# Attention stage of a graph network kernel: order of the first loads on SP, and the engine that clears the accumulator

## The chip, the cores and the metric

One core of a Trainium2 chip runs the whole program in one launch. The metric is the device time of that launch in microseconds: the median of three runs is 8271.29 us (8269.59 to 8273.54).

## The reference, cut to what matters

The program computes a layer stack on 6250 nodes of 256 features and 200,000 edges: a heterogeneous graph attention, a mixing branch, a routed feed-forward part, then a graph convolution, a linear attention and a mixture of experts. The change lies in the edge part of the first of these:

```python
q_att = jnp.einsum('nhd,rhde->rnhe', q, relation_att)
v_msg = jnp.einsum('nhd,rhde->rnhe', v, relation_msg)
aw_q_edge = q_att[etype, col_idx]
msg_edge = v_msg[etype, row_idx]
attn_score = jnp.sum(aw_q_edge * k[row_idx], axis=-1)
score = attn_score * (relation_pri[etype] / SQRT_DK)
m = jax.ops.segment_max(score, col_idx, num_segments=n)
ex = jnp.exp(score - m[col_idx])
denom = jax.ops.segment_sum(ex, col_idx, num_segments=n)
alpha = ex / denom[col_idx]
agg = jax.ops.segment_sum(alpha[..., None] * msg_edge, col_idx, num_segments=n)
```

The kernel folds the relation matrices into a table with one row for each relation and source node (keys and values, 2 KB a row), so each edge gathers one row of that table and is multiplied with the query of its target node. Edges are sorted by target.

## The kernel before, in words

The program is a row of stages (function `stage`), each followed by a barrier of all engines (line 3014 in the profile) and the clearing of its semaphores. The stage before the changed one, `node_tables`, writes the table and the queries to HBM. The changed stage is `attention_edges`; after it come `merge_carried` and `after_attention`.

`attention_edges` works on 208 groups (GROUPS) of 8 tiles (G) of 128 edges. Four slots (SLOTS) hold groups in flight: group k uses slot k mod 4. Targets are held in 50 blocks (NB) of 126 nodes, and all 50 blocks of queries (`qb`, 128 x 256 f32 each, 128 KB) and of accumulators (`acc`, 128 x 13300 f32 in all) stay in SBUF.

- **SP** loads. Lines 1026 and 1027: the block numbers of all steps (`blocks`, every second of 1664 integers, 832 pieces of 4 bytes, written over the start of `step_sums`). Line 1029: the fifty blocks of queries. Line 1031 (`chunk_load`): the edge columns of 16 groups at a time (192 KB), double-buffered. Lines 1039 and 1043 (`rows`): for each group the places of its edges, broadcast to 128 partitions (`oht`, 512 KB), and a mask (32 rows of 129 f32). A row load waits for the expansion of the group that last used its slot, a mask load for its weighting.
- **POOL** clears `acc` (line 1069) and then issues the gathers (line 1065), eight a group, 128 rows of 2 KB each. Each group's gathers wait for its index copy on ACT; from the fifth group on, every second gather also waits for one of the four summed pairs of the group four before it (`sum_made`), because they share a slot.
- **ACT** goes through a fixed order (`in_turns`): for a position k it does the copies and the store of group k-1's sums, the exponents and the one-hot places of group k, then `columns` and `mark` of group k+1, `indices` of group k+4 and `nodes` of group k+3. So before the loop the order is indices 0; indices 1, nodes 0; indices 2, nodes 1; columns 0, mark 0, indices 3, nodes 2. `mark` (lines 1192 and 1193) waits for the scores of its group. `indices` is line 1216, the sum copies are line 1173.
- **PE** waits for all queries (`q_in`, 50 loads) and for the packed block numbers (`packed_ready`), then goes through look-ups, expansions (line 1252: one-hot times query block, 16 matmuls a group), transposes of scores (1261) and of maxima (1269, 1270), and sums (line 1283, 16 matmuls in four pairs). An expansion waits for the node places of its group and for DVE's multiply of the group before.
- **DVE** first negates a column (1148), waits for `cleared` and for `blocks_in`, packs the block numbers (lines 974 to 977) and signals PE (1152). Then for each group: multiply gathered keys by expanded queries (line 1108, waits for all eight gathers and the expansion), reduce to scores (1130), two scans for the running maximum (1117, 1121), weights (1135), weighted values (1144), and the four additions into `acc` (line 1102) of the group before.

Of the kernel before, what the change touches and what calls it, by code (L numbers as in the profile page):

```python
# [20 lines left out]
P = 128  # L21
# [5 lines left out]
NB = 50  # L27
BW = 126
# [951 lines left out]
def attention_edges(nc, sem, psum, bank, c, dram):  # L980
# [3 lines left out]
    with ExitStack() as ctx:  # L984
# [6 lines left out]
        qb = sbt("q", [P, NB, D])  # L991
# [31 lines left out]

        @block.sync
        def _(sp):
            sp.dma_start(blocks, dram["blocks"].rearrange("(m x) -> m x", x=2)[:, 0:1].rearrange("m x -> x m"),
                         allow_slow_non_contiguous=True).then_inc(blocks_in, 16)
            for b in range(NB):
                sp.dma_start(qb[:, b, :], dram["q"][b * BW:b * BW + P, :]).then_inc(q_in, 16)
            def chunk_load(n):  # L1030
                sp.dma_start(chunk[:, (n % 2) * CHUNK:(n % 2 + 1) * CHUNK].rearrange("p k c g -> p (k c g)"),
                             dram["cols"][:, n * CHUNK:(n + 1) * CHUNK].rearrange("p k c g -> p (k c g)")
                             ).then_inc(chunk_in, 16)

            def rows(i):
                for s in range(SLOTS):
                    k = i * SLOTS + s
                    wait_count(sp, expanded[s], i)
                    sp.dma_start(oht[:, s, :], dram["rel_rows"][bass.ds(k * G, G)].rearrange("g n -> (g n)")
                                 .unsqueeze(0).broadcast_to([P, G * P])).then_inc(rows_in[s], 16)  # L1040

                    wait_count(sp, weighted[s], i * 2)
                    sp.dma_start(mk[:, s, :], dram["mask"][bass.ds(k * G, G)].rearrange("g h n -> (g h) n")
                                 ).then_inc(loaded[s], 16)
            chunk_load(0)
            for n in range(GROUPS // CHUNK):
                first = n * CHUNK // SLOTS
                rows(first)
                if n + 1 < GROUPS // CHUNK:
                    sp.wait_ge(chunk_in, 16 * n + 16)  # L1050

                    wait_count(sp, col_ready, CHUNK * n)
                    wait_count(sp, index_ready, CHUNK * n)
                    chunk_load(n + 1)
                with sp.Fori(first + 1, first + CHUNK // SLOTS) as i:
                    rows(i)
            sp.wait_ge(sum_added, GROUPS * PACK)
            for a, b in ((0, 112), (112, BW)):
                sp.dma_start(dram["sums"][0:NB * BW].rearrange("(b p) n -> p b n", p=BW)[a:b], acc[a:b]).then_inc(acc_stored, 16)
            sp.wait_ge(acc_stored, 32)  # L1060

        @block.gpsimd
        def _(g):
            def gather(i, s, n):
                g.indirect_dma_start(out=kv[:, s, n, :], out_offset=None, in_=dram["table"],  # L1065
                                     in_offset=bass.IndirectOffsetOnAxis(ap=index[:, s, n:n + 1].bitcast(U32), axis=0)
                                     ).then_inc(gathered[s], 16)

            g.memset(acc[:], 0.0).then_inc(cleared, 1)
            for s in range(SLOTS):  # L1070
                g.wait_ge(index_ready, s + 1)
                for n in range(G):
                    gather(0, s, n)
            with g.Fori(1, ITER) as i:
                for s in range(SLOTS):
                    g.wait_ge(index_ready, i * SLOTS + s + 1)
                    for n in range(G):

                        if n % 2 == 0:
                            g.wait_ge(sum_made, ((i - 1) * SLOTS + s) * PACK + n // 2 + 1)  # L1080
                            wait_alone(g, gate)
                        gather(i, s, n)

        @block.vector
        def _(v):
            def turn(i, s, scores, rest, adds):

                iz, sz = i + (s + 1) // SLOTS, (s + 1) % SLOTS
                ia, sa = i + (s - 1) // SLOTS, (s - 1) % SLOTS
                if adds:  # L1090
                    ka = ia * SLOTS + sa
                    at = blocks_of(v, packed, ka)

                def add(n):
                    if not adds:
                        return
                    v.wait_ge(sum_copied, ka * PACK + n + 1)

                    if n or not isinstance(ka, int) or ka:
                        v.wait_ge(sum_added, ka * PACK + n)  # L1100
                    o = acc[:, bass.ds(at[n], 1), :].rearrange("p b n -> p (b n)")
                    v.tensor_tensor(o, o, step_sums[:, n, :], ALU.add).then_inc(sum_added, 1)  # L1102

                if scores:
                    wait_after(v, gathered, iz, sz, per=16 * G)
                    wait_after(v, expanded, iz, sz)
                    k_ = kv[:, sz, :, 0:D]
                    v.tensor_tensor(k_, k_, psum[:, 0:4, :].rearrange("p b (t d) -> p (b t) d", d=D),  # L1108
                                    ALU.mult).then_inc(multiplied[sz], 1)
                if rest:  # L1110
                    wait_after(v, turned, i, s)
                    v.wait_ge(col_ready, i * SLOTS + s + 1)
                    wait_after(v, loaded, i, s, per=16)

                    wait_after(v, back, i, s, 1)
                    st = bank[6][0:G * H, 0:P]
                    v.tensor_tensor_scan(fwd[:], mk[:, s, 0:P], st, NEG, ALU.add, ALU.max).then_inc(swept[s], 1)
                add(0)
                if rest:
                    wait_after(v, swept, i, s, per=2, less=1)  # L1120
                    v.tensor_tensor_scan(mx[:, ::-1], mk[:, s, 1:P + 1][:, ::-1], fwd[:, ::-1], NEG, ALU.add, ALU.max
                                         ).then_inc(swept[s], 1)
                add(1)
                if rest:
                    wait_after(v, swept, i, s, per=2)
                    v.tensor_tensor(diff[:], st, mx[:], ALU.subtract).then_inc(maxed[s], 1)
                if scores:
                    wait_after(v, multiplied, iz, sz)
                    wait_after(v, turned, iz, sz, SLOTS)
                    v.tensor_reduce(sc[:, sz, :], kv[:, sz, :, 0:D].rearrange("p g (h d) -> p g h d", d=DK), AX.X, ALU.add  # L1130
                                    ).then_inc(scored[sz], 1)
                add(2)
                if rest:
                    wait_after(v, back, i, s)
                    v.tensor_tensor(kv[:, s, :, KC + C_M:KC + C_EX],
                                    bank[6][:, P:P + G * H].rearrange("p (g h) -> p g h", h=H),
                                    col[:, s, 1, :].unsqueeze(2).broadcast_to([P, G, H]), ALU.mult).then_inc(weighted[s], 1)
                add(3)
                if rest:
                    wait_after(v, factors, i, s)  # L1140

                    wait_after(v, exps, i, s)
                    vv = kv[:, s, :, D:2 * D].rearrange("p g (h d) -> p g h d", h=H)
                    v.tensor_tensor(vv, vv, bank[7][:, G * H:2 * G * H].rearrange("p (g h) -> p g h", h=H).unsqueeze(3)  # L1144
                                    .broadcast_to([P, G, H, DK]), ALU.mult).then_inc(weighted[s], 1)

            ch = Chain(v, pack_chain)
            v.tensor_scalar(less_p[:], c["pcol"][:], -1.0, None, ALU.mult).then_inc(place_ready, 1)
            v.wait_ge(cleared, 1)
            v.wait_ge(blocks_in, 16)  # L1150
            pack_blocks(v, ch, blocks, packed_f, packed)
            v.tensor_copy(diff[0:1, 0:1], packed_f[:, 0:1]).then_inc(packed_ready, 1)
            turn(-1, SLOTS - 1, True, False, False)
            for s in range(SLOTS):
                turn(0, s, True, True, s > 0)
            with v.Fori(1, ITER - 1) as i:
                for s in range(SLOTS):
                    turn(i, s, True, True, True)
            for s in range(SLOTS):
                turn(ITER - 1, s, s + 1 < SLOTS, True, True)  # L1160
            turn(ITER, 0, False, False, True)
# [1932 lines left out]
```

## Time and profile before

| | |
|---|---|
| median of three runs | 8271.29 us |
| the profiled execution | 8273.5 us |
| its span, first to last instruction | 8271.8 us |
| mean granted TensorE clock | 0.822 |
| busy PE / DVE / ACT / POOL | 70% / 57% / 43% / 44% of the span |
| attention stage | from 852.25 us to the next stage's first work at 3089.40 us |

Times in the profile are microseconds from the start of the span; durations of single instructions are in ns where a row says "mean ns". In a timeline a row is: start, length (of several equal ones together), engine, line, operation, what it writes and reads, count, and in brackets how long the engine was idle before it and what ended that. SPq, ACTq and POOLq are the sequencers that issue transfers. A row of waits is: who waited, for whom, total us, times, longest. A row of stretches is: stretch, its length, then the busy time and count of PE, weight loads, DVE, ACT and POOL, the granted clock as a share of 2.4 GHz, the busy share of the 16 DMA engines and GB/s. DMA queue q1 carries what SP issues, q0 what POOL issues.

### The profile page before, as it was taken

The page shows a single profiled execution, that of the slowest core. Times are in us where ns is not written, and L with a number is a line of the kernel's source. Part 1 is how long each engine was busy: PE and PEld are TensorE (multiplying, and loading weights), DVE is VectorE, ACT ScalarE, POOL GpSimd, SP SyncE. Part 2 cuts the span into 40 slices and gives each one's busy share as a digit, 9 for nine tenths or more (in the row PEclk, how much of TensorE's full clock was granted, in tenths as well). Part 3 has the DMA queues.
Part 4 walks back from the last instruction along what each step waited for, and adds up shares of the span by engine and source line. Part 5 has one row for each costly group of instructions (what it writes and reads, how often), then busy time and mean ns, then how long its engine had stood idle before and what let it go on. Part 6 is the DMA issues. An engine that isn't in the chain of part 4 may idle for free. (4 is left out here: it accounts for less than half of the span.)

```text
span 8271.8 us, 122585 instructions
## 1 busy us (share of the span) xinstructions
PE 5780.7 (70%) x31102; PEld 4434.8 (54%) x31103; DVE 4736.4 (57%) x11348; ACT 3572.6 (43%) x9149; POOL 3624.3 (44%) x3761
## 2 busy tenths in 40 slices
PE   2999688788777752699465655555534564499999
PEld 2555465555555541488444444444423444288888
DVE  5555688888888864522433334444429997433333
ACT  0554577777777750112111111111107998133333
POOL 1221677777777741501477777777750000000000
PEclk7999899999999985889656665555558988599999
DMA  6554788888888861512311111122232222200000
GB/s 145 205 212 196 230 258 259 259 259 260 258 258 259 259 186 47 176 42 70 100 26 26 26 26 37 45 45 45 47 50 76 79 80 63 93 13 13 13 12 10
DMA packets 487748, 984.74 MB, mean 119 GB/s; under 512 B 116003, under 2 KB 275273, under 8 KB 480612
## 3 DMA queue, kind: packets, MB, share of 16 engines
q0 software_dynamic: 216416, 661.87, 26.6%
q1 hardware_dynamic: 247406, 298.35, 12.2%
q10 hardware_dynamic: 23680, 21.44, 0.8%
q8 instruction: 130, 2.13, 0.1%
q14 instruction: 116, 0.95, 0.0%
HBM read 785.43 MB, written 203.65 MB: 120 GB/s over the span
## 5 line engine op out<-in xcount | busy, mean ns | idle before, releaser
L1065 POOL DMA_INDIRECT ae_kv<-edge_table,ae_index x1664 | 1629.5, 979 | 525.7 <-issue 470.3
L2119 POOL DMA_INDIRECT g_row<-y,g_index x1664 | 1599.3, 961 | 527.9 <-issue 506.5
L2138 PE MATMUL psum<-g_row,g_hot 128*128 128x64 f32 x3328 | 670.8, 386 | 833.3 <-issue 765.1
L2138 PEld LDWEIGHTS psum<-g_row,g_hot 128*128 128x128 f32 x3328 | 650.1, 298 | 872.3 <-issue 789.2
L1283 PE MATMUL psum<-ae_kv,ae_edge_hot 128*128 128x266 f32 x3328 | 859.4, 402 | 330.1 <-DVE ae_kv L1144 294.3
L1283 PEld LDWEIGHTS psum<-ae_kv,ae_edge_hot 128*128 128x128 f32 x3328 | 601.8, 190 | 580.4 <-issue 377.1
L1252 PE MATMUL psum<-ae_q,ae_node_hot 128*128 x3328 | 781.3, 388 | 67.4 <-ACT ae_node_hot L1232 36.0
L1252 PEld LDWEIGHTS psum<-ae_q,ae_node_hot 128*128 128x128 f32 x3328 | 621.1, 192 | 166.8 <-issue 88.1
L2944 ACT ACTIVATE em_h<-psum,em_affine 128x256 f32<-128x256 f32 x800 | 408.6, 561 | 625.8 <-PE psum L2896 441.6
L2299 DVE TENSOR_TENSOR g_acc<-g_acc,g_step_sums 128x64 f32 x832 | 188.7, 227 | 719.2 <-ACT g_step_sums L2215 490.2
L1108 DVE TENSOR_TENSOR ae_kv<-ae_kv,psum 128x2048 f32<-128x2048 f32 x208 | 475.8, 2287 | 208.3 <-DMA ae_kv<-edge_table,ae_index 204.5
L2683 ACT ACTIVATE gn_place<-iota,gn_ends 128x128 f32<-128x128 f32 x1664 | 528.3, 496 | 32.3 <-DMA gn_ends<-edge_ends 32.3
L1202 ACT ACTIVATE ae_edge_hot<-iota,ae_col 128x128 f32<-128x128 f32 x1664 | 508.9, 388 | 53.4 <-issue 53.1
L2998 DVE SCALAR_TENSOR_TENSOR em_o<-psum,em_weights,em_o 128x256 f32<-128x256 f32 x400 | 175.1, 479 | 576.3 <-PE psum L2916 571.3
L2862 POOL DMA_DIRECT2D out<-em_o x24 | 17.4, 726 | 1097.7 <-DVE em_o L2998 1097.7
L1144 DVE TENSOR_TENSOR ae_kv<-ae_kv,psum 128x2048 f32<-128x2048 f32 x208 | 474.2, 2280 | 0.0
L1130 DVE TENSOR_REDUCE ae_scores<-ae_kv 128x32 f32<-128x2048 f32 x208 | 470.8, 2264 | 0.0
L1173 ACT ACTIVATE ae_step_sums<-psum 128x266 f32<-128x266 f32 x832 | 318.1, 388 | 302.2 <-PE psum L1283 297.3
L2196 ACT ACTIVATE g_index<-g_ends 128x8 int32 (+1 forms) x208 | 43.2, 208 | 914.5 <-DMA g_row<-y,g_index 798.6
L2721 DVE SCALAR_TENSOR_TENSOR gn_picked<-iota,gn_tile,psum 128x100 f32<-128x100 f32 x1664 | 398.6, 310 | 55.1 <-PE psum L2772 54.8
L1102 DVE TENSOR_TENSOR ae_acc<-ae_acc,ae_step_sums 128x266 f32 x832 | 351.1, 422 | 78.1 <-issue 60.0
L2215 ACT ACTIVATE g_step_sums<-psum 128x256 f32<-128x256 f32 x208 | 80.0, 385 | 712.6 <-PE psum L2138 706.0
(545 smaller groups left out, 11248.4 us busy)
## 6 DMA issues: line engine op xcount, KB each, us to landing
ae_node_hot<-rel_rows SPq DMA_DIRECT2D x208, 512.0 KB, 5.6
gn_row<-source_places SPq DMA_DIRECT2D x208, 256.0 KB, 3.3
ae_kv<-edge_table,ae_index POOLq DMA_INDIRECT x1664
g_row<-y,g_index POOLq DMA_INDIRECT x1664, 2.4
x_sorted<-nt_x SPq DMA_DIRECT2D x52, 128.0 KB, 2.0
xt_kept<-nt_xt SPq DMA_DIRECT2D x52, 128.0 KB, 2.1
aa_xr<-x_sorted SPq DMA_DIRECT2D x52, 128.0 KB, 2.5
aa_xs<-xt_kept SPq DMA_DIRECT2D x52, 128.0 KB, 3.3
```

Source lines behind the costliest of these rows:

```text
L1065: g.indirect_dma_start(out=kv[:, s, n, :], out_offset=None, in_=dram["table"], in_offset=bass.IndirectOffsetOnAxis(ap=index[:, s, n:n + 1] ...
L1108: v.tensor_tensor(k_, k_, psum[:, 0:4, :].rearrange("p b (t d) -> p (b t) d", d=D), ALU.mult).then_inc(multiplied[sz], 1)
L1130: v.tensor_reduce(sc[:, sz, :], kv[:, sz, :, 0:D].rearrange("p g (h d) -> p g h d", d=DK), AX.X, ALU.add).then_inc(scored[sz], 1)
L1144: v.tensor_tensor(vv, vv, bank[7][:, G * H:2 * G * H].rearrange("p (g h) -> p g h", h=H).unsqueeze(3) .broadcast_to([P, G, H, DK]), ALU.mu ...
L1202: a.activation(ohs[:, n, :], c["iota"][:], ACT.Square, bias=col[:, s, 0, n:n + 1], scale=-1.0).then_inc(edge_far[s], 1)
L1252: ins = t.matmul(bank[n // 2][:, (n % 2) * D:(n % 2 + 1) * D], oht[:, s, n * P:(n + 1) * P], qb[:, bass.ds(at[n // 2], 1), :].rearrange("p ...
L1283: ins = t.matmul(bank[4 + m % 2][:, 0:CW], ohs[:, n, :], kv[:, s, n, KC:2 * D], start=n % 2 == 0, stop=n % 2 == 1)
L2119: g.indirect_dma_start(out=row[:, m, n, :], out_offset=None, in_=table, in_offset=bass.IndirectOffsetOnAxis(ap=index[:, m, n:n + 1].bitcas ...
L2138: ins = t.matmul(bank[m][:, n // 2 * W:(n // 2 + 1) * W], hot[:, m, n, :], row[:, m, n, :], start=n % 2 == 0, stop=n % 2 == 1)
L2683: a.activation(place[:, k % S, n, :], c["iota"][:], ACT.Square, bias=ends[:, k, 1, n:n + 1], scale=-1.0).then_inc(far, 1)
L2721: v.scalar_tensor_tensor(picked[:, k % S, n], c["iota"][:, 0:NT].unsqueeze(1).broadcast_to([P, W, NT]), tile[:, k, n:n + 1], bank[k % 2 * ...
L2944: ins = a.activation(h[:, f % 2, cc, :], bank[b + f % 2][:, cc * 2 * P:(cc + 1) * 2 * P], ACT.Relu, bias=affine[:, layer, 1, k:k + 1], sca ...
```

## The change

On SP the first chunk load is issued first, then the block numbers, then the rows and masks of the first four groups, then the fifty query loads; the loop over chunks leaves out the first call of `rows`. POOL no longer clears `acc`; DVE clears it after the packing and the signal to PE, and then waits for that clearing before the first turn.

```diff
         def _(sp):
-            sp.dma_start(blocks, dram["blocks"].rearrange("(m x) -> m x", x=2)[:, 0:1].rearrange("m x -> x m"),
-                         allow_slow_non_contiguous=True).then_inc(blocks_in, 16)
-            for b in range(NB):
-                sp.dma_start(qb[:, b, :], dram["q"][b * BW:b * BW + P, :]).then_inc(q_in, 16)
             def chunk_load(n):
...
+            chunk_load(0)
+            sp.dma_start(blocks, dram["blocks"].rearrange("(m x) -> m x", x=2)[:, 0:1].rearrange("m x -> x m"),
+                         allow_slow_non_contiguous=True).then_inc(blocks_in, 16)
...
-            chunk_load(0)
+            rows(0)
+            for b in range(NB):
+                sp.dma_start(qb[:, b, :], dram["q"][b * BW:b * BW + P, :]).then_inc(q_in, 16)
             for n in range(GROUPS // CHUNK):
                 first = n * CHUNK // SLOTS
-                rows(first)
+                if n:
+                    rows(first)
...
         def _(g):
...
-            g.memset(acc[:], 0.0).then_inc(cleared, 1)
...
         def _(v):
...
             v.tensor_scalar(less_p[:], c["pcol"][:], -1.0, None, ALU.mult).then_inc(place_ready, 1)
-            v.wait_ge(cleared, 1)
             v.wait_ge(blocks_in, 16)
             pack_blocks(v, ch, blocks, packed_f, packed)
             v.tensor_copy(diff[0:1, 0:1], packed_f[:, 0:1]).then_inc(packed_ready, 1)
+            v.memset(acc[:], 0.0).then_inc(cleared, 1)
+            v.wait_ge(cleared, 1)
             turn(-1, SLOTS - 1, True, False, False)
```

## Rows read from the trace of the kernel before

**Rows 1.** The page's groups, busy us and mean ns, then idle before
```profile
L1065 POOL DMA_INDIRECT ae_kv<-edge_table,ae_index x1664 | 1629.5, 979 | 525.7 <-issue 470.3
```

**Rows 2.** Waits from 930 to 3050 us
```profile
POOL ae_kv L1065 <- issue: 460.0, 1510, 0.3
...
DVE ae_kv L1108 <- DMA ae_kv<-edge_table,ae_index: 170.3, 195, 5.8
```

**Rows 3.** Timeline from 845 to 935 us, up to the first gather
```profile
852.25 0.59 SPq L1026 DMA_DIRECT2D ae_step_sums<-step_blocks  x1
852.25 11.18 POOL L1069 MEMSET ae_acc<- 128x13300 f32 x1 [11.18 <-POOLq L3014]
...
852.88 24.38 SPq L1029 DMA_DIRECT2D ae_q<-queries  x50
...
865.77 0.14 DVE L1152 COPY ae_diff<-ae_step_sums 1x1 f32<-1x1 f32 x1
877.29 0.43 SPq L1031 DMA_DIRECT2D ae_chunk<-edge_columns  x1
...
882.05 0.31 ACT L1216 ACTIVATE ae_index<-ae_chunk 128x8 int32<-128x8 int32 x2 [43.40 <-DMA ae_chunk<-edge_columns]
882.53 0.99 POOL L1065 DMA_INDIRECT ae_kv<-edge_table,ae_index  x1 [19.10 <-ACT ae_index L1216]
882.57 0.65 SPq L1031 DMA_DIRECT2D ae_chunk<-edge_columns  x1
```

**Rows 4.** The same timeline, from the first expansion to the fifth group's first gather
```profile
885.93 5.33 PE L1252 MATMUL psum<-ae_q,ae_node_hot 128*128 x16 [35.96 <-ACT ae_node_hot L1232]
...
891.35 0.95 POOL L1065 DMA_INDIRECT ae_kv<-edge_table,ae_index  x1 [0.30 <-issue]
...
897.33 2.29 DVE L1108 TENSOR_TENSOR ae_kv<-ae_kv,psum 128x2048 f32<-128x2048 f32 x1 [31.43 <-DMA ae_kv<-edge_table,ae_index]
...
902.19 0.19 ACT L1216 ACTIVATE ae_index<-ae_chunk 128x8 int32<-128x8 int32 x1
...
915.56 0.37 ACT L1173 ACTIVATE ae_step_sums<-psum 128x266 f32<-128x266 f32 x1
...
922.86 0.94 POOL L1065 DMA_INDIRECT ae_kv<-edge_table,ae_index  x1 [0.30 <-issue]
```

**Rows 5.** Loads into the chunk buffer, issue to landing
```profile
DMA to landing us min/median/max: 3.7/4.3/7.6
```

**Rows 6.** The page's DMA issues, KB each
```profile
ae_node_hot<-rel_rows SPq DMA_DIRECT2D x208, 512.0 KB, 5.6
...
ae_q<-queries SPq DMA_DIRECT2D x50, 128.0 KB
```

**Rows 7.** Clearings on DVE, by shape, busy us and mean ns
```profile
L2268 DVE MEMSET g_acc<- 128x3200 f32 x1 | 2.7, 2725 | 6.6 <-PEq L3014 6.6
...
L2730 DVE MEMSET gn_pair<- 128x1024 f32 x1 | 0.9, 912 | 1.6 <-PEq L3014 1.6
```

**Rows 8.** Five stretches: busy times, granted clock, DMA share, GB/s
```profile
852.00:859.00 7.00, 0.00 (x0) 0.00 (x0) 0.15 (x1) 0.00 (x0) 6.75 (x1) 0.72 0.82 84
859.00:867.00 8.00, 0.00 (x0) 0.00 (x0) 2.27 (x6) 0.00 (x0) 4.43 (x1) 0.50 1.08 345
867.00:881.00 14.00, 0.00 (x0) 0.00 (x0) 0.00 (x0) 0.00 (x0) 0.00 (x0) 0.50 0.90 269
...
884.00:890.00 6.00, 4.07 (x11) 3.36 (x12) 0.00 (x0) 4.05 (x6) 4.57 (x5) 0.56 1.04 388
890.00:896.00 6.00, 1.26 (x6) 0.76 (x4) 0.00 (x0) 0.00 (x0) 4.68 (x5) 1.00 0.92 301
```

**Rows 9.** DMA queues from 884 to 890 us: packets, MB, share
```profile
q1 hardware_dynamic: 578, 1.33, 60.4%
q0 software_dynamic: 289, 0.98, 42.1%
```

**Rows 10.** DMA queues from 884 to 887 us
```profile
q1 hardware_dynamic: 410, 1.10, 99.4%
q0 software_dynamic: 4, 0.02, 1.3%
```

## The prediction

> **What bounds the kernel now.** I read the page's table of costly groups first, then the waits inside the attention stage, then the timeline of its first 80 us, and last the DMA rates. The first shows the costliest group of the whole program, 1664 gathers on POOL, 979 ns each with about 0.3 us of issue in between [rows 1]. The waits from 930 to 3050 us say who paces whom: POOL's own entry is its issue, never over 0.3 us at a time, and DVE's multiply waits for gathers 195 times in 202 groups [rows 2]. DVE thus has 0.87 us to spare in each group and can catch up. So from the first gather to the last the stage is paced by POOL: 1.25 us per gather, 10 us and a little per group of eight. A microsecond by which the whole train of gathers starts earlier is a microsecond off the stage, and nothing follows in this program that would give it back, since every stage ends in a barrier. The start of the stage is the only place that the change touches. There the timeline shows POOL clearing the accumulator (11.18 us, from 852.25), SP issuing fifty query loads (24.38 us) and only then the chunk; the chunk lands at 882.05 and the first gather starts at 882.53 [rows 3]. At first sight 25 us are to be had.
>
> **What decides is not the first gather but the fifth group's.** The rows of the first groups [rows 4] show why. POOL can run three groups ahead on its own: the first three index copies on ACT need only the chunk and the first rows. The fourth index copy stands behind mark(0), which waits for the scores of group 0; it ran at 902.19, 4.9 us after the first multiply at 897.33. The fifth group reuses slot 0, so its first gather waits for the first summed pair of group 0, which ACT reads at 915.56; the release is just before that, 18.0 us after the first multiply. Before the change POOL gets to the fifth group at 922.86 [rows 4] and finds that release 7.5 us old. So with M for the start of the first multiply, the fifth group after the change starts at the later of POOL's own arrival and M + 18.0. Before, M = 897.33 was set by the last gather of group 0 (issued at 891.35, landing 6 us later), while the expansion was over at 885.93 + 5.33 = 891.3.
>
> **The change part by part.**
> *Chunk first.* It is issued at 852.25. The lightest landing of a chunk in the trace is 3.7 us after issue and ACT to POOL takes 0.5 us more [rows 3, 5]: first gather at about 856.5, 26 us earlier. The other end is the 4.8 us of the loaded queue, 857.6. Neither decides, as follows.
> *POOL's memset goes.* It ended at 863.4, with POOL idle for 19.1 us after it: worth nothing before, but now it would have been in the way of gathers from 856.5. On POOL its removal is part of that same 26 us.
> *DVE's memset comes.* No row shows DVE clearing 13300 columns. From the rows of 1024 and 3200 columns (912 and 2725 ns, 0.83 ns a column) I estimate 11.1 us [rows 7]; as bound from above I take twice that. It stands behind the packing, whose signal to PE it does not delay, and ahead of the first multiply. Packing was over at 865.9, 2.5 us after POOL's memset let it start [rows 3]; now it starts when the blocks have landed, at the latest at 863.4 and more likely near 859. DVE is free by 877 on the estimate, by 889 with the doubled bound. The first multiply comes later than both (below), so I cost it at nothing; with that cover gone it would cost its excess over M one to one. The added wait on DVE is for its own memset, and only the first multiply is behind it.
> *Blocks and rows ahead of the queries.* SP issues chunk, blocks (0.59 us) and four pairs of rows and masks (4.8 us for eight DMAs, between the two chunk loads at 877.29 and 882.57, the pairs by the code), then the queries in 24.4 us: the last query is issued at about 882.5 instead of 877.3. The rows land early and the node copies on ACT are done well before they are wanted. The second chunk moves from 882.57 to about 883; it is for the seventeenth group, so costs nothing. Rows for the next groups wait for expansions as before.
> *Queries against gathers.* PE waits for all fifty queries before its first expansion. Before, they had the DMA engines to themselves and were all in before the first gather. Now 24 gathers of 0.262 MB (128 rows of 2 KB, by the code) want 0.209 MB/us from 857 to 887, beside them. This is the term that decides, and the trace has no row with queries and gathers together.
>
> Bytes: SP's queue carries four rows of 0.524 MB, four masks of 0.017 (by the code) and fifty queries of 0.131 [rows 6]: 8.72 MB; the gathers bring 6.29 MB, together 15.01 MB. Queries alone ran at 345 GB/s while there was a backlog (859 to 867) and then at 269, which is just the pace of SP's issue, 0.131 MB each 0.488 us [rows 3, 8]. In both runs of the queue the blocks' 832 pieces of four bytes come early: from 852 to 859 only 84 GB/s moved [rows 8]. I take full traffic from 858.5.
>
> What do both queues carry together? From above: 388 GB/s, the six microseconds in which rows, chunk and gathers overlapped, with both queues well served [rows 8, 9]. From below: 301 GB/s, the next six, when it was gathers and one row. I take 370, nearer to the upper, since queries alone already did 345 and since the lower window was not always loaded. The gathers keep their 0.209, the queries' queue gets 0.161: 4.83 MB in the 30 us to 888.5. The remaining 3.89 MB go at 0.345: 11.3 us more, 899.8, and one for the last landing: 900.8. The first expansion takes 5.33 us as before: PE has been idle since before 852, and the granted clock was 0.50, the 1.2 GHz level, for it [rows 8]. So M = 906.2, 8.9 us later than before although the gathers started 26 us sooner. POOL, which stood still from 887, gets the fourth index at M + 5.3 = 911.5, issues the fourth group until 921.5 and waits for M + 18.0 = 924.2. Before it was 922.86: **+1.3 us**. The break-even is M = 904.9, queries in by 899.5.
>
> The Trainium skill ("DMA: Bandwidth & Descriptors", section "Issuing engines are not separate DMA queues") says that transfers issued from SP and from POOL run on the same 16 DMA engines and interleave. It speaks against the change, and the trace agrees: between 884 and 890 the two queues split the engines' time, 60% and 42% [rows 9]. The same page, section "Where 436 GB/s comes from", puts the HBM side of one core at about 358 GB/s; by that, as an estimate, 15.01 MB take 41.9 us and the queries are in at 901.4 with the landing, +1.9 us instead of +1.3; the measured 388 lies above the figure, so the sum goes by rows.
>
> **Time.** The profiled execution took 8273.5 us for a span of 8271.8; the median of the three runs is 8271.29, 2.2 lower. 8273.5 + 1.3 = 8274.8 in its own terms, 8272.6 against the median.
>
> **Rivals.**
> *SP's queue is served first (0.15).* Then the queries come as if alone: 8.72 MB at 0.345 is 25.3 us, in by 884.8 with the landing, M = 890.2, fifth group at 908.2: -14.7 us, 8257. For it: from 884 to 887 the gathers' queue moved 0.02 MB, though three gathers had been issued, while SP's queue was full [rows 10]. Against: of the 0.98 MB in the six microseconds [rows 9], 0.96 then moved in the last three, while a mask and a chunk were still in flight, so the delay looks like the depth of a queue more than like a rank. It decides from queries in before 899.5 on.
> *The mixture is slow (0.20), the one on the slower side.* Place: the same 50 query loads; price: their landing. At 301 GB/s the gathers leave 0.092: 2.76 MB in 30 us, 5.96 left, 17.3 us at 0.345: in at 906.8, M = 912.2, fifth group at 930.2: +7.3 us, 8279. If the rest runs only at 0.269, it is 910.7 plus landing, M = 917.1, +12.2 us, 8283. It decides from queries in later than 899.5.
> *The whole head start counts (0.02).* The fifth group would start at 896.9, -26 us, 8245. That wants M = 878.9, but SP issues the last query only at 882.5. All but excluded; a change that does nothing in the trace is as good as excluded, since the order of one queue is what the code says.
> The forecast with its neighbours, -4 to +5 us, has 0.61; 0.02 is for something else.
>
> **How the numbers follow.** A measurement of this kernel can tell about 0.2%, 16.5 us, from no change. Of the served-first case only its best corner passes that (0.03), with the whole head start 0.02: faster 0.05. Of the slow mixture only its tail passes it on the other side (0.02), with a bit for the unforeseen 0.01: slower 0.03; the same 0.92. The range of 8 in 10 reaches from just under the served-first value, 8256, to just over the slow mixture's 8279: 8256 to 8280, leaving the tails of both outside.
>
> **What the profile after would show.** Right: first gather near 857; 24 gathers without a gap, then POOL idle for some 24 us until an index copy; first expansion near 901 and first multiply 5.4 us behind it; a second, short idle of POOL before the fifth group, whose first gather is near 924; DVE's memset near 11 us in DVE's idle time. Total rates near 370 GB/s from 859 to 889. Wrong in size: first expansion at 885 (served first) or at 907 (slow mixture). Wrong altogether: DVE's multiply waiting for its own memset, the fifth group's gathers waiting for neither index nor sum, or a steady state with another period than 10.3 us a group; a tenth of a microsecond there would be 21 us.

## The result: faster, and outside the forecast's range

| | before | after |
|---|---|---|
| median | 8272.38 us (8269.59 to 8273.54, 4 runs) | 8224.26 us (8221.17 to 8228.56, 4 runs) |
| profiled execution, its span | 8273.5, 8271.8 | 8222.16, 8220.4 |
| first gather | 882.53 | 857.07 |
| first multiply | 897.33 | 904.55 |
| fifth group's first gather | 922.86 | 922.16 |
| last gather of the stage | 3017.69 | 2967.74 |
| next stage's first work | 3089.40 | 3040.72 |

The ratio is 0.9943, with a 95% interval of 0.9925 to 0.996. The forecast was 8272.6 us with a range of 8256 to 8280. The time is 48 us less than before, and the table shows where it is: not at the start of the stage, where the change lies. At the fifth group the new kernel is 0.7 us ahead, at the last gather 49.95 us. Between these two stand 203.875 groups, so a group takes 10.275 us before (2094.83 us in all) and 10.034 after (2045.58).

The start of the stage, in the timeline of the kernel after, from 845 to 935 us; the lines answer to [rows 3] and [rows 4]:

```profile
852.08 0.33 SPq L1027 DMA_DIRECT2D ae_chunk<-edge_columns  x1
...
857.07 0.99 POOL L1068 DMA_INDIRECT ae_kv<-edge_table,ae_index  x1 [16.28 <-ACT ae_index L1219]
857.39 35.14 SPq L1047 DMA_DIRECT2D ae_q<-queries  x50
...
863.17 11.14 DVE L1154 MEMSET ae_acc<- 128x13300 f32 x1 [2.72 <-issue]
...
899.12 5.29 PE L1255 MATMUL psum<-ae_q,ae_node_hot 128*128 x16 [49.32 <-DMA ae_q<-queries]
904.55 2.29 DVE L1110 TENSOR_TENSOR ae_kv<-ae_kv,psum 128x2048 f32<-128x2048 f32 x1 [30.23 <-PE psum L1255]
...
909.87 0.94 POOL L1068 DMA_INDIRECT ae_kv<-edge_table,ae_index  x1 [22.68 <-ACT ae_index L1219]
...
922.16 0.95 POOL L1068 DMA_INDIRECT ae_kv<-edge_table,ae_index  x1 [2.58 <-PE psum L1286]
```

The reader is to see the forecast's sequence here: gathers from 857, the queries' landing holding PE until 899, and POOL idle twice (22.68 us for an index copy, 2.58 us for the first summed pair).

The rest of the stage is in two views. The page's group of the gathers after (answering to [rows 1], 1629.5 us and 979 ns before):

```profile
L1068 POOL DMA_INDIRECT ae_kv<-edge_table,ae_index x1664 | 1580.1, 950 | 547.8 <-issue 501.1
```

And the waits from 930 to 3050 us after (who waited, for whom, total us, times, longest), answering to [rows 2]:

```profile
POOL ae_kv L1068 <- issue: 490.7, 1610, 0.3
...
DVE ae_acc L1104 <- ACT ae_step_sums L1176: 115.4, 209, 3.9
...
DVE ae_kv L1110 <- DMA ae_kv<-edge_table,ae_index: 9.8, 3, 4.4
```

Before, DVE's multiply waited for gathers 195 times, 170.3 us in all. After, it does so 3 times, and what DVE waits for instead is ACT's copy of the sums, 209 times. POOL still waits for little but its issue; its gathers themselves are shorter, by 49.4 us in sum. That is the whole gain.

### The profile page after: what moved, and what is told of

Read it like the earlier page. It is cut to its first block and busy times, and to the rows that moved or that the text cites. A ratio compares the mean times of both kernels' runs of the same rounds, so it can differ in the third digit from the quotient of the medians.

```text
span 8220.4 us, 122584 instructions
## 1 busy us (share of the span) xinstructions
PE 5759.5 (70%) x31102; PEld 4432.7 (54%) x31103; DVE 4750.2 (58%) x11349; ACT 3539.3 (43%) x9149; POOL 3566.5 (43%) x3760
## 5 line engine op out<-in xcount | busy, mean ns | idle before, releaser
L1068 POOL DMA_INDIRECT ae_kv<-edge_table,ae_index x1664 | 1580.1, 950 | 547.8 <-issue 501.1
L1255 PE MATMUL psum<-ae_q,ae_node_hot 128*128 x3328 | 777.9, 387 | 52.4 <-DMA ae_q<-queries 49.3
L1176 ACT ACTIVATE ae_step_sums<-psum 128x266 f32<-128x266 f32 x832 | 300.3, 386 | 323.3 <-PE psum L1286 317.1
```

Source lines behind the costliest of these rows:

```text
L1255: ins = t.matmul(bank[n // 2][:, (n % 2) * D:(n % 2 + 1) * D], oht[:, s, n * P:(n + 1) * P], qb[:, bass.ds(at[n // 2], 1), :].rearrange("p ...
```

## Where a long gather comes from

The timelines of both kernels near 1500 us show it. I call **lag** the time from the end of a group's last gather on POOL to the start of its multiply on DVE (medians over groups 20 to 190: 2.79 us before, 5.62 after). Before, in POOL's and in DVE's timeline from 1495 to 1508 us:

```profile
1497.54 0.95 POOL L1065 DMA_INDIRECT ae_kv<-edge_table,ae_index  x1 [0.30 <-issue]
1498.79 0.95 POOL L1065 DMA_INDIRECT ae_kv<-edge_table,ae_index  x1 [0.30 <-issue]
...
1503.79 1.21 POOL L1065 DMA_INDIRECT ae_kv<-edge_table,ae_index  x1 [0.30 <-issue]
...
1501.24 2.29 DVE L1108 TENSOR_TENSOR ae_kv<-ae_kv,psum 128x2048 f32<-128x2048 f32 x1 [0.82 <-DMA ae_kv<-edge_table,ae_index]
...
1503.78 0.40 DVE L1102 TENSOR_TENSOR ae_acc<-ae_acc,ae_step_sums 128x266 f32 x1
...
1504.54 0.44 DVE L1102 TENSOR_TENSOR ae_acc<-ae_acc,ae_step_sums 128x266 f32 x1
```

After, same window:

```profile
1503.68 0.95 POOL L1068 DMA_INDIRECT ae_kv<-edge_table,ae_index  x1 [0.31 <-issue]
...
1500.21 2.28 DVE L1110 TENSOR_TENSOR ae_kv<-ae_kv,psum 128x2048 f32<-128x2048 f32 x1
...
1503.35 0.43 DVE L1104 TENSOR_TENSOR ae_acc<-ae_acc,ae_step_sums 128x266 f32 x1 [0.54 <-ACT ae_step_sums L1176]
...
1504.15 0.43 DVE L1104 TENSOR_TENSOR ae_acc<-ae_acc,ae_step_sums 128x266 f32 x1
```

Before, the group's last gather ends at 1498.49, the multiply starts 2.75 us later, and an addition into `acc` starts 2.54 us after that, within 0.01 us of the start of the next group's fifth gather. That gather takes 1.21 us instead of 0.95. As the multiply waits for its gathers in nearly every group (195 of 202), this meeting comes again and again. After, the lag is 5.60 us, the additions start 0.33 us before and 0.47 us after the gather's start, and it takes 0.95.

Counting all gathers that start from 950 to 2950 us, by whether an addition of DVE starts between 0.25 us before and 0.15 us after the gather's start:

| | with such an addition | mean | without | mean |
|---|---|---|---|---|
| before | 194 | 1.197 us | 1362 | 0.949 us |
| after | 21 | 1.000 us | 1574 | 0.948 us |

The 194 gathers of before carry 47.9 us over 0.95 each, nearly the whole gain. Among them the excess grows with the addition's offset: 0.11 us on average where it starts 0.20 to 0.15 us before the gather, 0.21 at 0.10 to 0.05 before, 0.27 at 0 to 0.05 after, 0.33 at 0.05 to 0.10 after. So excess = offset + about 0.25. With an addition of 0.40 us that is what one gets if the gather needs something of SBUF 0.15 us after its start and is held until the addition is over; this reading is worked out from the offsets, no row shows it directly. The addition reads both inputs from SBUF, the gather reads its indices there.

The window is not the whole rule. Behind the first scan (line 1117) an addition that starts as late as 0.28 us after the gather still holds it, by up to 0.55 us: 10 such gathers of before lie outside the table. And of the 194, 11 are not held at all. In each of these an addition that does not stand behind that scan starts between 0.03 us before and 0.12 after the gather; the gather takes 0.95 us, and it is the addition that can be long, up to 0.50 us where it takes 0.44 otherwise. One of them, in the timeline of before from 1538 to 1541 us:

```profile
1539.54 0.48 DVE L1102 TENSOR_TENSOR ae_acc<-ae_acc,ae_step_sums 128x266 f32 x1 [0.26 <-issue]
1539.55 0.95 POOL L1065 DMA_INDIRECT ae_kv<-edge_table,ae_index  x1 [0.30 <-issue]
```

The Trainium skill ("SBUF — State Buffer", section "Who interferes with whom") says that a DVE instruction with two SBUF inputs contends with a GpSimd instruction that reads SBUF, and that the order of issue decides which of the two is blocked. The trace agrees on the pair, and on either side being held, 1.197 us against 0.95 for the gather and 0.48 against 0.44 for the addition. Which of the two it is cannot be told from the recorded starts alone, as the additions behind the first scan show.

**Theory A (phase).** The loop has two periods. At a lag of 2.75 us an addition meets one gather a group, at 5.6 us almost none; the change only makes the loop start at a larger lag, because POOL now has to wait for DVE's sums before the fifth group (lag 7.35 us there, 3.08 before). **Theory B**: the gain comes from what was moved, the clearing on DVE or the first loads, in themselves. **Theory C**: from the earlier start.

## Experiments

### Parts of the change, full computation

e1 is the kernel after with the clearing back on POOL, e2 the kernel before with the clearing on DVE, e3 the kernel before with DVE cleared for longer, so that its first multiply is late, e4 the kernel before without the additions (the sums over the edges are left out, a clearing of 532 columns stands in the place of each). The edits are cut to the lines that matter; with its clearing e1 also moves DVE's wait for `cleared` back, and each clearing of e3 is waited for.

```diff
 e1  POOL +            g.memset(acc[:], 0.0).then_inc(cleared, 1)
     ...
     DVE  -            v.memset(acc[:], 0.0).then_inc(cleared, 1)
     ...
 e3  DVE  +            v.memset(acc[:], 0.0).then_inc(cleared, 1)     # three times
     ...
     DVE  +            v.memset(acc[:, 0:25, :], 0.0).then_inc(cleared, 1)
 e4  DVE  -                    v.tensor_tensor(o, o, step_sums[:, n, :], ALU.add).then_inc(sum_added, 1)
     DVE  +                    v.memset(acc[:, 0:2, :], 1.0).then_inc(sum_added, 1)
```

> The order of loads of the change, with the clearing still on POOL, so the first gather comes at 863.5 instead of 857. Theory A (phase): after the change the first multiply is late (904.55) against gathers that end early, the lag from a group's last gather to its multiply settles at 5.6 us instead of 2.75, and there no gather runs long; period 10.03 us a group instead of 10.28. It needs only the late first multiply, so this kernel is as fast as the changed one: 8220 to 8230 us. Theory B (engine of the clearing: something of POOL's memset slows its gathers): 8260 to 8280. Theory C (head start of the gathers counts one to one): 6.5 us slower than the changed kernel, 8231.

> DVE clears the accumulator, the order of loads is that of before. Theory A: the first gather and the first multiply stay at 882.5 and 897.3 and so does the lag of 2.75 us: 8268 to 8276 us, period 10.28. Theory B: period 10.03, 8220 to 8230. Theory C: 8272.

> The kernel before with nothing but a delay: DVE clears the accumulator three and a half times more before its first multiply, which so comes at about 905 instead of 897. Theory A: the gathers are ahead by 12 us at the first group as they are after the change, the lag settles near 5.6 us, period 10.03, and the kernel gets FASTER by the added delay: 8218 to 8230 us. Theories B and C: nothing is gained, 8272 or up to 8 us slower, 8272 to 8280.

> The kernel before, with DVE's four additions a group into the accumulator (two inputs from SBUF) replaced by memsets of 532 columns, which read nothing and are a little longer; the sums are left out of the computation. Theory A in its full form (a gather runs long where its descriptor writing meets such an addition): no gather over 1.0 us, period 10.03 although the lag stays near 2.75, 8215 to 8225 us. If the long gathers come from something else that is tied to the lag (the transfers, the waits on sums), they stay: 1.2 to 1.3 us for one gather in eight, 8265 to 8280 us.

They ran on a chip on which the kernel before takes 9198.51 us, not 8272 (a long-landing chip from here on, that of the result being a short-landing one). Ratios to it: e1 0.9994 (0.9985 to 1.0004), e2 1.0003 (0.9994 to 1.0013), e3 1.0011 (1.0002 to 1.0021), e4 0.9999 (0.999 to 1.0009). The waits of e1 from 930 to 3050 us show why nothing is told apart ("remote" stands where the profile does not show what ended the wait):

```profile
DVE ae_kv L1111 <- remote: 471.4, 156, 4.7
POOL ae_kv L1068 <- PE psum L1286: 363.5, 149, 2.7
POOL ae_kv L1068 <- issue: 355.3, 1095, 1.9
```

On that chip a group's multiply starts some 14 us after its last gather was issued (2.75 before), a group takes 12.45 us, and POOL waits for the sums of the group four before. By the code the multiply waits for the gathers and for the expansion, and the expansion had ended 4.1 us (median) before the multiply started; so I take it that the landing of the gathers paces the loop, though no row shows a landing. Where POOL waits anyway, a longer gather costs nothing: the gathers of e1 take 1604.6 us in sum and those of e4, without any addition, 1585.2, yet e4 gains nothing. The same four on another chip, which proved to be of the same kind (before 9290.47 us):

> The same kernel as e1_loads_only, because that run met a chip on which the kernel before takes 9198 us and a gather needs 14 us to land, so that the transfers pace the stage and no phase between engines can show. On a chip where before takes about 8272: theory A (phase) 8220 to 8230 us, theory B (engine of the clearing) 8260 to 8280, theory C (head start one to one) 8231. On the other kind of chip: within 0.1% of before again.

> The same kernel as e2_clear_only. On a chip where before takes about 8272: theory A 8268 to 8276 us with a period of 10.28 us a group; theory B 8220 to 8230; theory C 8272.

> The same kernel as e3_late_dve: before, with only DVE's first multiply held back to about 905. On a chip where before takes about 8272: theory A 8218 to 8230 us, faster by the delay, period 10.03; theories B and C 8272 to 8280.

> The same kernel as e4_adds_no_reads; DVE's additions into the accumulator are left out, memsets of 532 columns stand in their place. On a chip where before takes about 8272: theory A in its full form no gather over 1.0 us and 8215 to 8225 us; if the long gathers come from the lag alone and not from what DVE reads, they stay and it takes 8265 to 8280.

f1 0.9979 (0.9965 to 0.9993), f2 1.0002 (0.9991 to 1.0013), f3 1.0003 (0.9991 to 1.0014), f4 1.0002 (0.9989 to 1.0015).

### Half rows

To make landing short on any chip, these kernels gather 1 KB for each edge instead of 2. The value half of the buffer is left out of the gathers and set to 1 once. The indices are left as they are while the table is cut into 1 KB pieces, so index i brings the i-th piece and not the keys of row i: number, issue and size of the gathers are those wanted, but neither scores nor values are the reference's.

```diff
-                g.indirect_dma_start(out=kv[:, s, n, :], out_offset=None, in_=dram["table"],
+                g.indirect_dma_start(out=kv[:, s, n, 0:D], out_offset=None, in_=dram["table"].rearrange("m (o n) -> (m o) n", o=2),
...
+            v.memset(kv[:, :, :, D:2 * D], 1.0)
```

h0 is before, h1 after, h3 is e3 and h4 is e4, each with this edit.

> The kernel before with half of each gathered row (1 KB instead of 2; the value half of the row is left out and set to 1 once), so that transfers land quickly on every chip while POOL issues as many gathers of 128 descriptors as ever. It is the reference for the next three. Theory A (phase): DVE catches up with the gathers, each group's multiply waits for its last gather, one gather in eight runs at 1.2 to 1.3 us, period 10.25 to 10.30 us a group. If the long gathers come from the load on the DMA engines, they are gone here and the period is 10.03.

> The changed kernel with the same half rows. Theory A: no gather over 1.1 us, multiply 5 to 6 us behind a group's last gather and waiting for none, period 10.03; 45 to 60 us less than h0_half_before. If the phase has nothing to do with it, the same period as h0_half_before and a difference of 5 to 25 us, by the start alone.

> h0_half_before with nothing but DVE's first multiply held back to about 912 by clearing the accumulator three and a half times more. Theory A: period 10.03 and 35 to 50 us FASTER than h0_half_before. Theory B (engine of the clearing) and theory C (head start one to one): not faster, 0 to 15 us slower.

> h0_half_before with DVE's additions into the accumulator left out, memsets of 532 columns that read nothing in their place. Theory A in its full form (a long gather is one whose descriptor writing meets an addition with two SBUF inputs): no long gathers although the multiplies wait for the gathers, period 10.03, 40 to 55 us less than h0_half_before. If it is the lag alone, the long gathers stay and the time is within 10 us of h0_half_before.

This chip was a short-landing one: the kernel before took 8286.16 us. Measured (8 runs of h0, 2 of h1, 4 of h3, 3 of h4):

| | time | ratio to before | first multiply | fifth group's first gather | last gather | us a group | steady lag |
|---|---|---|---|---|---|---|---|
| h0 | 8303.01 | 1.0023 (1.0011 to 1.0034) | 900.27 | 927.22 | 3044.49 | 10.385 | 1.84 |
| h1 | 8225.7 | 0.9925 (0.9896 to 0.9953) | 902.60 | 921.80 | 2967.36 | 10.033 | 5.62 |
| h3 | 8252.36 | 0.9963 (0.9944 to 0.9983) | 926.40 | 947.95 | 2993.65 | 10.034 | 5.62 |
| h4 | 8236.18 | 0.9938 (0.9915 to 0.996) | 899.55 | 928.47 | 2973.90 | 10.033 | 1.84 |

(us a group: last gather less fifth group's first, over 203.875. Steady lag: median over groups 20 to 190.)

**h3 against h0** decides against C. Nothing in h3 is early: its loads are before's, POOL clears as before, and its first multiply is 26.1 us later than h0's. It is 50.7 us faster. So POOL is made to wait for the fifth group's release here too (6.54 us before its first gather at 947.95), by another means, and the lag settles at the same 5.62 us. The first multiply came later than the 912 expected, because each long clearing has 2.8 us of issue ahead of it. Half of the gathered bytes (h0 against before) brought nothing either. The waits of h3 from 1000 to 2900 us have no entry of DVE's multiply, and those of h0 do:

```profile
POOL ae_kv L1065 <- issue: 461.8, 1516, 0.3
...
DVE ae_acc L1102 <- ACT ae_step_sums L1182: 104.4, 189, 0.6
```

```profile
DVE ae_kv L1108 <- DMA ae_kv<-edge_table,ae_index: 163.2, 176, 2.2
```

**h4** tells meeting from lag, and decides against B: it has neither part of the change and gains 66.8 us against h0, more than the 40 to 55 expected, since in h0 nearly two gathers a group are held and not one. Its lag is h0's, 1.84 us in both, yet its period is the short one: a clearing of 532 columns stands in the place of each addition and reads nothing. The pairs in the timelines, first h0 (POOL, then DVE), where two gathers a group are held:

```profile
1502.07 0.94 POOL L1065 DMA_INDIRECT ae_kv<-edge_table,ae_index  x1 [0.30 <-issue]
1503.32 1.05 POOL L1065 DMA_INDIRECT ae_kv<-edge_table,ae_index  x1 [0.30 <-PE psum L1284]
...
1505.92 1.18 POOL L1065 DMA_INDIRECT ae_kv<-edge_table,ae_index  x1 [0.30 <-issue]
...
1503.11 0.44 DVE L1102 TENSOR_TENSOR ae_acc<-ae_acc,ae_step_sums 128x266 f32 x1
...
1505.86 0.41 DVE L1102 TENSOR_TENSOR ae_acc<-ae_acc,ae_step_sums 128x266 f32 x1
```

and h4, first with a clearing that starts 0.12 us before a gather and does not lengthen it, then with the longest gather of the stage (timelines from 1076 to 1079 and from 1183 to 1185 us):

```profile
1077.14 0.50 DVE L1102 MEMSET ae_acc<- 128x532 f32 x1 [0.20 <-DVE ae_acc L1102]
1077.26 0.95 POOL L1065 DMA_INDIRECT ae_kv<-edge_table,ae_index  x1 [0.30 <-issue]
...
1183.49 0.50 DVE L1102 MEMSET ae_acc<- 128x532 f32 x1
1183.52 1.52 POOL L1065 DMA_INDIRECT ae_kv<-edge_table,ae_index  x1 [0.31 <-PE psum L1284]
1183.93 0.35 DVE L1121 TENSOR_TENSOR_SCAN ae_max<-ae_mask,ae_fwd 32x128 f32<-32x128 f32 x1
```

The clean comparison leaves out what stands behind the first scan. In h0, 318 gathers have such an addition starting 0.25 to 0.05 us before them, and every one is long, 1.04 to 1.21 us; in h4, 17 have a clearing there, and every one takes 0.94 or 0.95. What is left in h4 is the second scan (line 1121), which also reads both inputs from SBUF: 35 of 1594 gathers take more than 1.02 us there, each of them beside it, most at 1.02 to 1.06 and six at 1.35 to 1.52. In sum they are small, 3.7 us over 0.947 each for the whole of h4 from 950 to 2950 us, against 72.2 in h0.

What is left is A: the period follows the meetings (h4), and a late release sets the lag at which they fall away (h3).

### One part alone, half rows, and another order

h5 is e1, h6 is e2 and h7 is after with e4's edit, all with half rows. n1 computes everything: it is the kernel after, with the rows of the last three slots behind the queries, and with the gathers held until 28 of the 50 queries have landed (its edit, cut to three places).

```diff
-            rows(0)
+            rows(0, (0,))
...
-                sp.dma_start(qb[:, b, :], dram["q"][b * BW:b * BW + P, :]).then_inc(q_in, 16)
+                sp.dma_start(qb[:, b, :], dram["q"][b * BW:b * BW + P, :]).then_inc(q_some if b < 28 else q_in, 16)
...
+            g.wait_ge(q_some, 16 * 28)
```

> Half rows as in h0_half_before, with the change's order of loads and the clearing still on POOL. Theory A (phase, entered by the late first multiply behind early gathers): period 10.03 us a group, lag 5.6, within 5 us of h1_half_after. If the clearing's move is needed: period 10.38 as in h0_half_before, 60 to 80 us more.

> Half rows, the order of loads of before, the clearing on DVE. Its clearing ends near 890, before the first multiply at 900, so theory A: lag 1.9 us, period 10.38, the time of h0_half_before within 5 us. If the clearing's move makes the gain: period 10.03, 60 to 80 us less.

> h1_half_after with DVE's additions left out, memsets of 532 columns in their place. If the additions are what holds the multiplies 5.6 us behind the gathers (they yield to the gathers there, as the gathers yield to them at 1.9), the lag now shrinks group by group to about 1.9 us, at a period of 10.03. If it is the chain of copies through ACT and PE, the lag stays between 5 and 6 us. The time is within 10 us of h1_half_after in both cases.

> Full rows, the whole computation. The changed kernel with the rows of the second to fourth group behind the queries, and the gathers held until 28 of the 50 queries have landed. Worked out as the prediction did: first gather at about 872, queries in by 888, first multiply at about 894.5 instead of 904.5, fifth group at 912.5 instead of 922.2, and the lag at the fifth group 7 us, so the fast phase: 8 to 12 us less than the changed kernel, about 8214 us where that takes 8224. If the lag at the start falls short of what the fast phase needs: period 10.28 and about 8265. On a chip where a gather takes 14 us to land: within 0.2% of before.

The chip was that of f1 to f4, a long-landing one (before 9282.82 us), and with half rows too the multiply started some 14 us after a group's last gather, so they did not do what they were made for; what made the table above conclusive was its chip. h5 0.9982 (0.9971 to 0.9994), h6 1.0001 (0.9989 to 1.0012), h7 0.9985 (0.9974 to 0.9996), n1 0.9988 (0.9976 to 0.9999). What they do show is what an early start is worth where landing paces the loop: the fifth group starts at 920.69 in h5 and at 941.18 in h6, 20.5 us apart, and the times are 21.8 us apart. The first multiply is the same in both (899.63 and 899.31), but in h6 the gathers of the second group were issued only from 894.96 on and are waited for until 930.17. The last two runs were e1 and n1 once more:

> The order of the loads alone, the clearing back on POOL, on what is hoped to be a chip where a group's gathers land some 3 us behind the last issue. There the clearing on POOL ends about 873, so that the first gather begins near 873 and not 857, the queries are in near 897 and the first multiply begins near 902; the fifth group's first gather near 920. Theory A: what matters is whether the multiply starts far enough behind the group's gathers that the additions fall away from them. In the changed kernel the lag at the fifth group is 7.35 us and settles at 5.6. Here three groups of gathers (30 us) also end at 903, before the first multiply is done, so the lag at the fifth group is again above 5.6: period 10.025 us, time within 10 us of the changed kernel (8215 to 8235). Theory B (DVE's clearing is what the change gains by): time of before, 8270 to 8290. If this chip is one where gathers land 14 us late: both within 0.3% of before, 9240 to 9300, and nothing is told apart.

> All of the change, and besides the queries ahead of the rows of three slots, gathers held until 28 of the 50 queries have landed. First gather near 872, first multiply near 894 to 906, fifth group's first gather near 912 to 926. Theory A: the lag decides the period; gathers start only some 25 to 30 us ahead of the first multiply, so three groups are still issued before it, the lag is above 5.6 and the period 10.025 us, and the time is the changed kernel's plus or minus what the fifth group's first gather moves against 922.16 (8214 to 8230). Rival: the lag at the fifth group is under 3 us, the multiply is limited by the gathers, period 10.28 and a time of 8260 to 8275. If gathers land 14 us late on this chip: 9240 to 9300, nothing told apart.

Before took 9266.43 us, g1 0.9987 (0.9977 to 0.9996), g2 0.9992 (0.9982 to 1.0001). In n1 and g2 holding the gathers back brought the queries in hardly sooner: first gather 872.58 and 871.24, but first multiply 906.64 and 904.55, against 908.15 and 908.32 in f1 and g1 on the same chips, where n1 had been expected some 10 us sooner than the change.

## Why the prediction was wrong

**Right: the start.** Its steps held nearly one by one. First gather 857.07 against 856.5. Queries in at 899.1 against 900.8, first multiply 904.55 against 906.2: from 867 to 881 us the two queues together moved 370 GB/s, the value taken. Fifth group's first gather 922.16 against 924.2, so +1.3 us became -0.7. The release came 17.6 us after the first multiply, 18.0 taken. Both idle times of POOL are there, 22.68 and 2.58 us. Two details were off and cost nothing: SP took 35.14 us to issue the queries and not 24.4, so the last one went out near 892.5 instead of 882.5; and the granted clock over the first expansion was 0.69 in both kernels, not 0.50. The rivals, served first, slow mixture and whole head start, all lay in this part, and none came true. DVE's clearing has the 11.14 us estimated from [rows 7] in its row, but DVE was taken 2.72 us longer by the "issue" ahead of it; at 874.3 it was over, 30 us before DVE was needed. As costed, it is hidden.

**Wrong: the rest of the stage.** The step that failed is "from the first gather to the last the stage is paced by POOL: 1.25 us per gather, 10 us and a little per group of eight", with "the start of the stage is the only place that the change touches". Paced by POOL is right, in both kernels. But the little over 10 us was taken as a constant, and it is a state of the loop: 0.24 us a group that is there at one lag of DVE behind POOL and gone at another. The change alters the lag at which the loop sets in, through the very wait that the forecast had worked out (POOL waits for the sums of group 0), and 203.875 times 0.2416 is 49.3 us. The text had its price ("a tenth of a microsecond there would be 21 us") and listed it as what would be altogether wrong, but gave it no chance of its own; only the 0.02 for something else was left for it.

**It could have been read.** The group has a mean of 979 ns [rows 1], and each single gather in [rows 4] 0.94 or 0.95. The 29 ns between them times 1664 are 48 us. A mean above the usual single value asks for the long ones; they stand beside DVE's additions, always in the same place of the group. The change leaves both instructions as they are and moves their engines against each other.

**What stays open.** Which of the two instructions waits at a meeting, beyond what the offsets show, is not settled. Nor is which part of the change alone sets the lag: the order of the loads alone ran four times and the clearing alone three, each time on a long-landing chip, where the loop is paced otherwise. By the trace it should be the order of the loads, because POOL then has three groups issued before the first multiply, but that is argued, not shown. Nor is it settled what holds the lag at 5.6 us for 190 groups. DVE then waits about 0.5 us a group for ACT's sums and never for gathers, so DVE does not catch up as the forecast supposed; why its loop through PE and ACT keeps exactly POOL's pace no run told. Whether n1 beats the change on a short-landing chip is not known, nor what the change itself is worth on a long-landing one: there the order of the loads alone gave 0.06% (within its interval) to 0.21%. No version was found that beats both kernels.

## What to carry to other kernels

In a loop of engines that run beside each other, compare the mean of the pacing instruction with its usual single value; if they differ, find what it meets, and count the difference times the number of calls as something that any shift of phase can give or take. Two engines that are locked to each other by a wait meet at the same place in every turn, so a contention of 0.25 us becomes a tax on all of them. And see by the landing which kind of chip a run had before it is read: where landing paces the loop, a phase is worth nothing and an early start what it says.

## What the runs showed of the hardware

- A kernel that starts its multiplies 26 us later ended 51 us earlier (h3 against h0).
- A gather of 128 rows takes 0.95 us on POOL. Where a DVE addition with two SBUF inputs starts 0.25 to 0.05 us before it, it took longer every time (64 of 64 in before, 321 of 321 in h0); where one starts up to 0.28 us behind, some gathers took up to 0.55 us more and some nothing. A scan with two SBUF inputs lengthens it too, to at most 1.52 us (h4).
- A clearing on DVE does not lengthen it: 17 of 17 gathers with one of 532 columns just before them take 0.94 or 0.95 us (h4), and so do those beside the one of 13300 columns, from 863 to 874 us (after).
- A clearing on DVE of 13300 columns has 11.14 us in its row and 2.72 to 2.84 us of issue ahead: three in a row in e3 start 13.98 us apart.
- SP needed 35.14 us to issue the fifty query loads beside gathers of 2 KB rows (after), 25.42 beside gathers of 1 KB (h1) and 24.38 alone [rows 3].
- Chips differ. On one kind a group's multiply can start 2.8 us after its last gather was issued (1.8 us with half rows), on the other some 14 us, with half of the bytes too (h5, h6); the same kernel takes 8272 to 8286 us on the one and 9199 to 9290 on the other.
